# A mixture of experts on one core: 63 tiles of 256 rows and nine of 128 in place of 71 of 256

## The reference

```python
h = tokens(...)                              # 64 x 128 tokens of 192 numbers, with graph features and a layer norm
h = h + long_convolution(layernorm(h))       # along the 128 positions
x = layernorm(h).reshape(8192, 192)
top2_values, top2 = top_k(x @ Wr.T, 2)       # 8 experts
share = softmax(top2_values)
expert_e(x) = gelu(x @ Wi[e].T + bi[e]) @ Wo[e].T + bo[e]      # 192 -> 768 -> 192
out = h + share[0] * expert_{top2[0]}(x) + share[1] * expert_{top2[1]}(x)
```

## Time and profile before

| what | value |
|---|---|
| time, median of 3 runs | 991.08 us (987.75 to 995.53) |
| profiled execution, first to last instruction | 995.9 us |
| TensorE / VectorE / ScalarE / GpSimd busy | 87% / 66% / 54% / 65% of the span |
| transfers | 138.31 MB |

### The profile page before, as it was taken

One profiled execution on the slowest core, in us unless ns is written; L12 is line 12 of the kernel. 1 busy time (PEld: TensorE's weight loads), 2 busy tenths in 40 slices (PEclk: granted clock), 3 DMA queues, 4 the chain that ended last, 5 costly groups with the idle time before them and its releaser, 6 DMA issues.

```text
span 995.9 us, 22850 instructions
## 1 busy us (share of the span) xinstructions
PE 869.3 (87%) x7469; PEld 822.9 (83%) x7469; DVE 656.0 (66%) x2142; ACT 536.0 (54%) x1271; POOL 644.7 (65%) x552
## 2 busy tenths in 40 slices
PE   3959898998898739893889999999999999999993
PEld 2959898998898738892679999999999989898993
DVE  3167857776867565978756776666667656666662
ACT  1222223213312325599667777777777767677761
POOL 6777777777777300100067886777778768788886
PEclk9957556556756669996699999999999999999997
DMA  8437547457465429855946446745744543343454
GB/s 245 131 87 248 179 153 257 136 200 225 157 207 195 126 86 282 225 166 131 245 101 149 61 60 158 191 61 122 199 83 63 130 96 61 59 60 59 61 57 44
DMA packets 99788, 138.31 MB, mean 139 GB/s; under 512 B 13427, under 2 KB 81430, under 8 KB 97654
## 3 DMA queue, kind: packets, MB, share of 16 engines
q0 software_dynamic: 39552, 53.26, 28.1%
q1 hardware_dynamic: 59142, 73.59, 24.3%
q10 hardware_dynamic: 1008, 10.34, 2.8%
HBM read 98.14 MB, written 39.02 MB: 138 GB/s over the span
## 4 chain that ended last, share of the span: by engine, by line
PE 29%; DMA 22%; POOL 22%; issue 12%; DVE 8%; ACT 4%; DVEq 2%; SPq 1%; POOLq 0%; ACTq 0%
DMA out<-Hs,id_s 20%; POOL ev_g L521 13%; POOL emb_g L512 5%; PE bank L799 3%; PE bank L801 3%; PE bank L800 3%; POOL blob L537 3%; PE bank L780 2%; PE bank L781 2%; PE bank L784 2%; PE bank L783 2%; PE bank L782 2%; DVE hstats L1157 2%; ACT adj_s L956 1%; PE bank L763 1%
## 5 line engine op out<-in xcount | busy, mean ns | idle before, releaser
L975 ACT ACTIVATE Hs<-bank,U 128x256 bf16<-128x256 f32 x426 | 214.0, 502 | 126.0 <-PE bank L784 126.0
L551 POOL DMA_INDIRECT out<-Hs,id_s x142 | 233.5, 1645 | 65.6 <-issue 45.6
L537 POOL DMA_INDIRECT blob<-xtab_d,id_g x142 | 151.6, 1068 | 122.7 <-DVEq L1340 79.6
L521 POOL DMA_INDIRECT ev_g<-in_word_emb,ids_i x192 | 189.7, 988 | 58.5 <-issue 57.9
L976 ACT ACTIVATE Hs<-bank,U 128x256 f32<-128x256 f32 x426 | 216.4, 508 | 0.0
L799 PE MATMUL bank<-U,Hs 128*128 128x192 bf16 x852 | 210.0, 246 | 0.3 <-issue 0.3
L801 PE MATMUL bank<-U,Hs 128*128 128x192 bf16 x852 | 208.8, 245 | 0.0
L800 PE MATMUL bank<-U,Hs 128*128 128x192 bf16 x852 | 208.5, 245 | 0.0
L1362 DVE TENSOR_TENSOR Hs<-Hs 128x512 bf16<-128x512 f32 x213 | 146.8, 691 | 92.1 <-ACT Hs L976 92.0
L780 PE MATMUL bank<-wst,U 128*128 128x256 bf16 x426 | 116.6, 274 | 1.3 <-DVE wst L1351 1.3
L781 PE MATMUL bank<-wst,U 128*128 128x256 bf16 x426 | 116.7, 274 | 0.0
(11 more groups left out here) (216 smaller groups left out, 1643.2 us busy)
## 6 DMA issues: line engine op xcount, KB each, us to landing
adj_s<-in_adj SPq DMA_DIRECT2D x48, 256.0 KB, 7.3
ev_g<-kpad_d SPq DMA_DIRECT2D x24, 512.0 KB, 5.8
U<-blob_d SPq DMA_DIRECT2D x14, 771.0 KB, 5.0
wst<-in_wsrc SPq DMA_DIRECT2D x8, 1344.0 KB
blob_d<-blob ACTq DMA_DIRECT2D x7, 1443.0 KB
U<-blob_d SPq DMA_DIRECT2D x14, 672.0 KB, 5.7
xtab_d<-U SPq DMA_DIRECT2D x4, 1552.0 KB, 17.0
out<-Hs SPq DMA_DIRECT2D x4, 1536.0 KB, 12.8
```

Of the source, the lines that this page charges most:

```text
L521: pool.indirect_dma_start(ev_g[:, p, j, b, :], None, t["word_emb"], bass.IndirectOffsetOnAxis(ap=ids_i[:, 1 + j, i * Q + b:i * Q + b + 1], ...
L537: pool.indirect_dma_start(xg_f[:, q % RX, h, :], None, xtab_d, bass.IndirectOffsetOnAxis(ap=id_g[:, 2 * q + h:2 * q + h + 1], axis=0)).the ...
L551: pool.indirect_dma_start(out, bass.IndirectOffsetOnAxis(ap=id_s[:, 2 * q + h:2 * q + h + 1], axis=0), yo[:, q % RY, h, :], None, compute_ ...
L975: f(hh[w][:, d, :], ps, ACT.Gelu, bias=bi[:, d:d + 1])
```

## The change

The slots are now cut into 135 blocks of 128 rows: `FULLS` = 63 tiles of two blocks and `SINGLES` = 9 tiles of one. Every expert has its whole pairs of blocks in the large tiles and, where its number of blocks is odd, one block in a small tile. The small tiles stand at fixed places: first of all, after 8, 16, 24, 32, 40, 48 and 55 large tiles, and at the end (tiles 0, 9, 18, 27, 36, 45, 54, 62 and 71 of 72). In a small tile the gather and the scatter are one indirect DMA each, the up matmuls have 128 columns, there are three transposes and 18 down matmuls, and the gelus and the copies have half the columns. Which rows a small tile holds is known only at run time; SyncE reloads weights by the same rule as before. The routing's arithmetic has more steps. The core of the diff:

```diff
-NT = (2 * B * S + E * (TS - 1)) // TS
-NC = NT * TS // 128
+NC = (2 * B * S + E * 127) // 128
+SINGLES = E + 1
+FULLS = (NC - SINGLES) // 2
+NT = FULLS + SINGLES
+SINGLE_AFTER = (0, 8, 16, 24, 32, 40, 48, 55, 63)
...
+def tile_order():
+    order, single = [], 0
+    for full in range(FULLS + 1):
+        for _ in range(SINGLE_AFTER.count(full)):
+            order.append((2 * FULLS + single, 1))
+            single += 1
+        if full < FULLS:
+            order.append((2 * full, 2))
+    return order
+TILES = tile_order()
+def blocks(q):
+    return range(TILES[q][1])
+def block_of(q, h):
+    return TILES[q][0] + h
+def width(q):
+    return 128 * TILES[q][1]
+def landed_by(h, q):
+    return 16 * sum(TILES[k][1] > h for k in range(q, -1, -2))
...
             def fetch(q):
                 after(pool, hid, q - RX + 1)
-                for h in range(2):
+                for h in blocks(q):
...
             def add_rows(q):
-                before = held[q] if q in held else landed_by(q - 1)
                 for h in range(2):
                     if q > 1:
-                        pool.wait_ge(scat[h][q % 2], landed_by(q - 2))
+                        after(pool, scat[h][q % 2], landed_by(h, q - 2))
                     if q > 0:
-                        pool.wait_ge(scat[h][(q - 1) % 2], before)
+                        after(pool, scat[h][(q - 1) % 2], held[h, q] if (h, q) in held else landed_by(h, q - 1))
                         pool.sem_inc(pool_turn, 1)
                 pool.wait_ge(yo_ready, q + 1)
-                for h in range(2):
+                for h in blocks(q):
...
-                x0, x1, x2 = (xgT[:, q % W3, c, :] for c in range(3))
+                x0, x1, x2 = (xgT[:, q % W3, c, 0:width(q)] for c in range(3))
...
-                        f(hh[w][:, d, :], ps, ACT.Gelu, bias=bi[:, d:d + 1])
-                        last = f(hf[w][:, d, :], ps, ACT.Gelu, bias=bi[:, d:d + 1])
+                        f(hh[w][:, d, 0:width(q)], ps, ACT.Gelu, bias=bi[:, d:d + 1])
+                        last = f(hf[w][:, d, 0:width(q)], ps, ACT.Gelu, bias=bi[:, d:d + 1])
...
-            v.tensor_scalar(cnti[:, 1, :], cnti[:, 0, :], 8, None, ALU.logical_shift_right)
...
-            v.scalar_tensor_tensor(sl, repeat(cnt[:, 3, :], 1, B), float(TS), bank[7][:, :].rearrange("p (b e) -> p b e", e=E), ALU.mult, ALU.add)
+            v.tensor_scalar(cnti[:, 1, :], cnti[:, 0, :], 7, None, ALU.logical_shift_right)
+            v.tensor_scalar(cnti[:, 2, :], cnti[:, 0, :], 8, None, ALU.logical_shift_right)
...
+            v.tensor_scalar(cnt[:, 0, :], cnt[:, 4, :], total, 2.0, ALU.add, ALU.mult)
+            v.tensor_tensor(beyond, place, repeat(edge[:, 0, :], 1, B), ALU.is_ge)
+            fence()
+            v.scalar_tensor_tensor(last_block[:, 1:E + 1], cnt[:, 4, :], pair_end, cnt[:, 0, :], ALU.add, ALU.min)
+            v.scalar_tensor_tensor(sl, repeat(edge[:, 1, :], 1, B), float(TS), place, ALU.mult, ALU.add)
+            fence()
+            v.scalar_tensor_tensor(cnt[:, 1, :], last_block[:, 0:E], 0.5, pairs_of, ALU.mult, ALU.subtract)
+            v.tensor_scalar(reached[:, 1, :], last_block[:, 1:E + 1], cst[:, 640:641], None, ALU.is_le)
+            fence()
+            v.tensor_tensor(beyond, beyond, repeat(cnt[:, 1, :], 1, B), ALU.mult)
+            v.tensor_reduce(eidr, reached.rearrange("p a e -> p (a e)"), AX.X, ALU.add).then_inc(experts_at, 1)
+            fence()
+            v.scalar_tensor_tensor(sl, beyond, float(TS), sl, ALU.mult, ALU.add)
```

More of the change, by code:

```diff
@@ L56 @@
 LATE = 8
+def tile_order():
[16 more added lines that the diff above has]
+    return 16 * sum(TILES[k][1] > h for k in range(q, -1, -2))
+assert len(TILES) == NT and 2 * FULLS + SINGLES == NC
+assert all(TILES[q][1] == 2 for q in range(NT - LATE - 1, NT - 1))
 def tower(nc, t, out):
@@ L224, in tower @@
         marks = sb("marks", [1, 3, LATE])
-        late = sb("late", [1, LATE], i32)
+        late = sb("late", [1, 2, LATE], i32)
+        expert_row = sb("expert_row", [1, 2, NT])
         tp = old_adj[:, 0:2 * CC * 128].rearrange("p (a c t) -> p a c t", a=2, c=CC)
@@ L340, in tower @@
         N_LOADS = 17
-        def landed_by(q):
-            return 16 * (q // 2 + 1)
         def store_expert(eng, e):
@@ L559, in _ @@
                 fetch(q)
-            held = {NT - LATE + k: pool.value_load(late[0:1, k:k + 1], min_val=landed_by(NT - LATE - 3), max_val=landed_by(NT - 2)) for k in range(LATE)}
+            held = {(h, NT - LATE + k): pool.value_load(late[0:1, h, k:k + 1], min_val=landed_by(h, NT - LATE + k - 3), max_val=landed_by(h, NT - LATE + k - 1))
+                    for h in range(2) for k in range(LATE)}
             pool.wait_ge(h_out, 16 * (NG + 1))
@@ L957, in _, with fetched_by @@
                 last.then_inc(hot_s_ready, 1)
+            def fetched_by(q):
+                return 16 * sum(TILES[k][1] for k in range(q, -1, -RX))
             def row_hi(q):
-                act.wait_ge(xg_in[q % RX], 32 * (q // RX + 1))
+                act.wait_ge(xg_in[q % RX], fetched_by(q))
                 after(act, xg_t, q - 1)
-                f(xs[:, q % 2, :, 0:D], xg_f[:, q % RX, :, 0:D], ACT.Copy).then_inc(x_hi, 1)
+                f(xs[:, q % 2, 0:TILES[q][1], 0:D], xg_f[:, q % RX, 0:TILES[q][1], 0:D], ACT.Copy).then_inc(x_hi, 1)
             row_hi(0)
@@ L1275, in _ @@
             fence()
[L1276 to L1280 removed]
+            ends, pairs_of, total = cnt[:, 2, :], cnt[:, 3, :], cnt[:, 3, E - 1:E]
@@ new lines, in _ @@
+            v.scalar_tensor_tensor(cnt[:, 4, :], pairs_of, -2.0, ends, ALU.mult, ALU.add)
+            v.tensor_scalar(pair_end, total, float(FULLS), total, ALU.max, ALU.add)
+            v.tensor_scalar(last_block[:, 0:1], total, 2.0, None, ALU.mult)
+            v.tensor_scalar(reached[:, 0, :], pairs_of, 2.0, cst[:, 640:641], ALU.mult, ALU.is_le)
+            v.tensor_tensor(edge[:, 1, :], pairs_of, cnt[:, 1, :], ALU.subtract)
+            fence()
+            v.tensor_scalar(cnt[:, 0, :], cnt[:, 4, :], total, 2.0, ALU.add, ALU.mult)
@@ L1361, in split_hidden @@
                     dve.wait_ge(gelu, FC // 2 * q + c // 2 + 1)
-                    last = v.tensor_tensor(hl[w][:, c:c + 2, :], hf[w][:, c:c + 2, :], hh[w][:, c:c + 2, :], ALU.subtract)
+                    last = v.tensor_tensor(hl[w][:, c:c + 2, 0:width(q)], hf[w][:, c:c + 2, 0:width(q)], hh[w][:, c:c + 2, 0:width(q)], ALU.subtract)
                 return last
             def bias_out(q):
-                w, x = q % W3, q % RY
-                for h in range(2):
-                    if q >= RY:
-                        dve.wait_ge(scat[h][q % 2], landed_by(q - RY))
+                w, x, n = q % W3, q % RY, TILES[q][1]
+                if q >= RY:
+                    for h in blocks(q - RY):
+                        dve.wait_ge(scat[h][q % 2], landed_by(h, q - RY))
                 dve.wait_ge(down, q + 1)
-                v.tensor_tensor(yo[:, x, :, :], bank[5 + w][:, 0:2 * D].rearrange("p (h d) -> p h d", h=2),
-                                repeat(parts(wbuf[q % WB])[5], 1, 2), ALU.add).then_inc(biased, 1)
+                v.tensor_tensor(yo[:, x, 0:n, :], bank[5 + w][:, 0:n * D].rearrange("p (h d) -> p h d", h=n),
+                                repeat(parts(wbuf[q % WB])[5], 1, n), ALU.add).then_inc(biased, 1)
                 fence()
-                for h in range(2):
+                for h in blocks(q):
                     last = v.tensor_scalar(yo[:, x, h, :], yo[:, x, h, :], wk[:, w, h:h + 1], None, ALU.mult)
```

72 lines of the change are left out of this document (43 added, 29 removed).

## The result

| | before | after |
|---|---|---|
| time, median of 20 runs each | 993.03 us (985.67 to 997.91) | 998.26 us (993.27 to 1006.32) |
| ratio to before | | 1.0063, 95% interval 1.0042 to 1.0084 |
| profiled execution, span | 995.9 us | 998.6 us |
| transfers | 138.31 MB | 147.26 MB |

Forecast were 990 us and "no change"; it is slower, by 0.4 to 0.8%. The time lies in the range. The ratio goes by the means, 992.6 and 998.9 us, which are 6.3 us apart; the medians are 5.2 us apart.

The account below looks back on a forecast made before the run. GpSimd's growing backlog was taken to set the end. Terms +2.6 + 0.5 - 21.1 + 14.9 + 3.5 + 2.3 - 1.5 gave +1.2, or -1.0 with reloads at 12.7; 991.1 - 1 gives 990 us, range 974 to 1002.

Parts of the forecast that it names:

- The opening: GpSimd's first gathers up to its first scatter: one gather less, first scatter at 514.9 us, 2.0 earlier; sum +0.5 us.
- The sum: All terms of the change added up: +1.2 us, or -1.0 with the lower reload term, carried to 990 us.
- The first half: The stretch from the start to the slots' first step: no change predicted, 0 us.
- Slots' arithmetic and tables: Routing steps ahead of the first gather: arithmetic +3.1 us, narrower tables -0.5 us, together +2.6 us.
- From first to last scatter: GpSimd's expert stage: seven blocks less at -21.1 us, against reloads, single gathers and backlog; these terms give -1.6 us.
- Reloads: GpSimd's waits beside extra weight reloads: 11 more touched tiles at 1.35 us, +14.9 us (3 to 23), or 12.7.
- A small tile's single gather: GpSimd gathering a small tile leaves 3.2 us against a landing of 3.7: 0.5 us for seven, +3.5 us (0 to 5).
- 0.8 us to spare: GpSimd between large tiles: 4.5 us pass before the next scatter, so a 3.7 us landing is hidden with this slack.
- The catching up: GpSimd's instructions need 6.44 us a tile, so beside small tiles it regains some backlog: -1.5 us (0 to -9).
- 3.3 us for a small tile: TensorE's time for a small tile, exactly half a large one; seven times this is -23 us there.
- The first (reloads cheap, or TensorE the bound, 973 to 983): Rival: reloads hardly count, 973 to 978 us, or TensorE sets the end, 977 to 983; chance 0.32 for below 981.
- The second: Rival: slower by GpSimd's reload waits, 2.1 us per further touched tile, +14 us, 1005 us; chance 0.15 for over 1%.

Follow-up runs that it names:

- early_loads: The kernel after with GpSimd's 16 register loads moved ahead of its wait for the first row list, their values computed some rounds earlier; ratio to before 0.9975.
- before_longer_arithmetic: The kernel before with three idle steps of 512 columns and some small ones added to the slots' arithmetic; ratio to before 1.0042.
- no_extra_reloads: The kernel after with every small tile run on its neighbour's weights (wrong expert for its rows), 14 reloads in place of 21; ratio to before 0.9987.
- before_held_everywhere: The kernel before with the landing wait left out from tile 5 on wherever tile and predecessor share an expert, register loads inside the loop; ratio to before 0.9908.
- after_held_everywhere: The kernel after, landing wait left out from tile 5 on behind large tiles of the same expert, register loads inside the loop; ratio to before 0.9761.
- before_16_loads: The kernel before with 16 register loads in place of 8 and nothing else; ratio to before 1.0028.

## Why the prediction was wrong

**The opening is the step that failed.** "GpSimd then issues 13 gathers ahead of its first scatter, not 14, which end at about 514.6": they ended at 523.3. Of these 8.7 us, 5.3 are the gap of the register loads, which the prediction doesn't have at all; 2.8 (of this execution; 2.3 in the mean) came from the first half and 0.5 from the arithmetic and the tables. The change added eight register loads on the sequencer of the engine that sets the end, and the working counted only its gathers and scatters. In the trace of before they showed as 0.44 us of idle time at one gather. Doubled, they outlasted the lead of the sequencer. early_loads took 8.8 us off, give or take 3.7, enough for the whole loss of 6.3. By its profile 4.0 of the 5.3 us that the opening misses are the loads; in the rest the gathers end and GpSimd stands idle for 1.60 us until tile 0 has its bias, where the prediction has its rows "ready in time".

**The sum.** It is 2.6 us too high, as the arithmetic is counted twice. Without that the forecast would have been 987.5 us, further off. That 998.26 us lies in the range is luck: the upper end stands for costly reloads, and they were cheap.

**The first half.** Predicted unchanged, +2.3 us in the means. It lies in the busy time of the gathers into `ev_g` and isn't explained; it is not the place of the buffers.

**Slots' arithmetic and tables.** +2.6 predicted, +3.1 measured; before_longer_arithmetic shows that it isn't hidden.

**From first to last scatter** the terms give -1.6 us and +0.9 were measured, and most of the terms are off. Reloads: +14.9 or 12.7 predicted, 7.6 measured (no_extra_reloads), 0.5 to 0.65 for a touched tile. 1.35 was read from three places of consecutive reloads in one execution, against a pace that was itself that of this execution; both executions of the kernel after show how far such places differ. A small tile's single gather: 0.5 each predicted. Of the eight small tiles that are gathered behind the opening, five have idle times of 1.36 to 1.64 us behind their single gather, 1.1 to 1.3 over the usual 0.3, and a sixth, beside a reload, 2.20 us. The gather for tile 9 came behind two others, and for tile 71 the wait was released. That makes 5.7 to 7.6 us against +3.5, beyond its upper end of 5. The reason is in the same rows: from the start of the second scatter, 851.07, to that of the next, 855.47, 4.4 us pass, not the 3.7 of the landing. In a tile of two gathers 4.5 us pass anyway, so the "0.8 us to spare" were hardly 0.2. The rest of the stretch (a backlog that begins at 7.8 us and not near 5, the pace beside a full backlog) is some 7 to 9 us, against 3 predicted with the returned idle time; no run separates it. Bias waited from tile 18, not 31.

**The catching up.** The prediction lets GpSimd, whose instructions need 6.44 us a tile, gain on TensorE's 6.59. The trace of before shows that it doesn't, even where it has a backlog and nothing is reloaded: its scatter follows the bias by 4.8 us from tile 6 to 11 and by 17.9 us from tile 32 to 38, so its step is 6.59 us too, with 0.3 us of idle time in front of each instruction. What makes it longer is one instruction a tile. VectorE's second row split and GpSimd's two gathers there:

```profile
761.06 0.41 DVE L1347 TENSOR_TENSOR wst<-blob,wst 128x256 bf16<-128x256 f32 x1
...
761.20 1.18 POOL L537 DMA_INDIRECT blob<-xtab_d,id_g  x1 [0.30 <-issue]
762.68 0.98 POOL L537 DMA_INDIRECT blob<-xtab_d,id_g  x1 [0.30 <-issue]
```

The gather that starts 0.14 us behind the start of the row split takes 1.18 us, its neighbour 0.98. At 570.07 (row split) and 570.21 (gather, 1.17 us) it is the same 0.14 us, though the backlog is 13 us smaller there, and in before_held_everywhere it is a scatter, 0.15 us behind (798.72 and 798.87), that takes 1.73 us where 1.59 is usual. So GpSimd falls into step with VectorE, and what a reload costs it isn't won back in these stretches. That the row split is what stretches the instruction is argued from these times; no run moves it alone.

**TensorE.** That it is not the bound after was right, and the only thing that kept its term, 3.3 us for a small tile, from mattering: it is 4.6, more than the 4 us that the prediction names as the sign of a wrong term. The 128-column matmuls have the 56 ns of the estimate. The Trainium skill (TensorE: Matmul & The Clock Gate, "Back-to-back issue gap") gives some 81 ns for them; this case's trace doesn't agree, in a stream of 30 with a weight load each.

**The rivals.** The first (reloads cheap, or TensorE the bound, 973 to 983) is what comes out, by TensorE, where the landing wait is mostly left out: after_held_everywhere, 972.11 us. The second had the right sign by the wrong term: touched tiles cost a third of what it needed, and the loads, which it doesn't have, came in their place. The Trainium skill (SBUF — State Buffer, "SBUF: two separate sides") was cited for a catching up of GpSimd beside small tiles; no run shows one. The stretched instructions above stand beside a VectorE subtraction; whether that is in such a mode no run shows.

## What to carry to other kernels

When an edit is priced on the engine that sets the end, count every instruction its queue gets, register loads too, and ask how far its sequencer is ahead there; a cost that is hidden at eight may be exposed at sixteen. A half-size tile saves half only where both halves of the saving fall into the same step and no fixed latency stands behind it. And take the wait away first: with the register loads out of the opening, the same change is worth 2.5 us, give or take 3.0, beside the landing wait, and 14.7, give or take 5.8, where the wait is mostly left out.

## What the runs showed of the hardware

- A register load on GpSimd's sequencer takes 0.58 us from one to the next (503.1 to 511.8 us for 16), and 16 of them held up the gathers by 5.3 us behind five gathers, by 4.4 us behind six (before_16_loads).
- After the start of a scatter the next one that waits for its landing began 4.3 to 4.6 us later, where the landing itself is given as 3.7 us.
- A gather took 1.17 to 1.18 us in place of 0.98 where it started 0.14 us behind the start of VectorE's second row split, at backlogs of 4.8 and of 17.9 us, and GpSimd's step was then TensorE's 6.59 us.
- 30 matmuls of 128 columns with a weight load each started 56 ns apart, at a granted clock of 1.00 (after_held_everywhere).
- With the same reloads two executions of one program differ by 7 us in the expert stage (463.8 and 471.0 us).
- Seven more reloads, 10 MB, cost 7.6 us, give or take 3.5, where scatters wait for each other; where they mostly don't, no cost was seen, and it is at most 4 us.
